# A transformer block on one core: the second attention with queries turned by DMA, its context prepared in the stage before, and an unrolled order

## The chip, the cores and the metric

The kernel runs on one core of a Trainium2 chip. The metric is device time in microseconds (us) of one execution; less is better. The core's engines run side by side, each through a queue of its own in program order, and wait for one another by semaphores: TensorE (PE, matmuls; PEld is its weight load), VectorE (DVE), ScalarE (ACT), GpSimd (POOL) and SyncE (SP), which here only issues DMAs. Sixteen DMA engines carry out all transfers.

## The reference, cut to what matters

The input is 32 batches of 256 rows by 256 numbers (x), and for each batch a context of 120 rows by 256. Four layers follow one another:

```python
x = x + tanh(g_xattn[0]) * attention_0(layernorm(x), ctx)          # with rope
x = x + tanh(g_ffn[0])   * mixture_of_8_experts(layernorm(x))      # top 2 of 8
x = x + tanh(g_xattn[1]) * attention_1(layernorm(x), ctx)          # gated
x = x + tanh(g_ffn[1])   * ternary_ffn_with_conv(layernorm(x))
```

The third one is rewritten. With 16 heads of 16 numbers it computes

```python
qn = layernorm(q) * qln_g + qln_b             # q is layernorm(x)
kk = (layernorm(ctx) * kvln_g + kvln_b) @ Wk.T;  vv = (the same) @ Wv.T
attn = softmax(q_heads @ k_heads.T / 4)       # q_ = qn @ Wq.T
y = attn @ v_heads
return (y * sigmoid(qn @ Wg.T + bg)) @ Wo.T
```

## The kernel before

`program` (the last function before the layouts) runs four blocks one after the other, each ended by a barrier of all engines: `attention_first`, `experts`, `attention_second`, `ternary_ffn`. P is 128, and a batch of 256 rows is held as two tiles of 128 rows. Where f32 precision is wanted from bf16 matmuls, an operand is split into a high bf16 half and the bf16 rest, and three products are summed (high by high, high by low, low by high): `halves`.

`attention_first` is unrolled over the batches (`unrolled`). Its queries and keys are turned by DMA transposes and the maxima are spread by a DMA.

`experts` works through 71 tiles of 256 sorted rows. SyncE loads a tile, transposes it by DMA into one of three buffers (`turn`, L1934 ff.), and stores results into `back_rows`. TensorE makes 54 bf16 matmuls for a tile (L2127). Between them, `early` loads and `prepare` get the weights of the next stages ready (in SBUF that lasts, `Early`).

`attention_second` (from L1207) handles one batch a period, in stages of a software pipeline: each engine has a hand-ordered list of pieces, and `at(k)` is the batch that entered k steps ago. `stepped` (L84) unrolls the first 8 steps, loops over pairs of batches, and unrolls the last 7. For one batch:

- SyncE loads x (`a_xa`, two buffers) and the places of its expert rows; GpSimd adds the two expert results of each row with four gathers (`indirect_dma_start`, L1359 and L1369). SyncE stores the sum to `x2_rows` (L1316) and loads it again as residual `a_xr` five steps later (L1304). It also loads the context (`a_ca`).
- VectorE computes the statistics of rows and context (L1489 to L1503), GpSimd the inverse root, VectorE the norm (L1529 rows, L1560 context).
- TensorE turns rows (four f32 transposes) and context (two, L1737); ScalarE scales them out of PSUM (L1458, L1401) and makes the high halves, GpSimd the low halves (L1342, L1344).
- TensorE makes queries (12 matmuls of 128x256), keys and values (6 of 120x512), gates (12). Queries and keys are laid out as `qx` and `kx`, 8 pairs of heads by 96 columns (high, high, low), by L1430, L1539, L1540 and L1432, L1542, L1543.
- TensorE turns `qx` in 16 transposes (L1666, L1676) and `kx` in 8 (L1672); ScalarE (L1453) and VectorE (L1551) copy the turned queries to `a_q`, VectorE the keys, masked for two heads (L1553, L1556).
- Eight pairs of matmuls `ms0` to `ms7` give the scores row by row, from which VectorE takes the negative maxima (the eight TENSOR_REDUCE). They are turned (L1651), copied by ScalarE (L1441, `mt`), and spread by VectorE over the eight pairs of heads in rows 96 to 127 of `a_q` (L1547). Eight pairs `sc0` to `sc7` then give scores less maxima, key by query, into two PSUM banks in turn; ScalarE takes each through Exp (the eight `a_probs`).
- 32 small matmuls multiply by the values (L1643, L1657), ScalarE copies (`raw`), TensorE turns back (L1705, L1709), VectorE divides by the sums (`a_of`), TensorE turns (`oT`), VectorE applies the gate (`a_ot`, L1513), TensorE projects with f32 `a_ot` and `wo` in 8 matmuls (in L1593, into `a_ps_a`), and VectorE adds the residual (L1474, `a_x`). SyncE stores.

`product` (L1589 ff.) issues all its matmuls from one line, so L1593 is queries, gates, keys and values, and projection; the output's name tells them apart (`a_ps_c`, `a_ps_d`, `a_ps_b`, `a_ps_a`).

## Time and profile before

| | us |
|---|---|
| median of 3 runs (lowest, highest) | 1911.04 (1910.23, 1912.43) |
| span of the profiled execution | 1909.9 |
| first attention, until its last store is issued | 0 to 507 |
| experts, until the last result is stored | to 973 |
| second attention | 974.7 to 1484.4 |
| ternary feed-forward | 1484.4 to 1909.9 |

The page of the profiled execution gives, over the whole span, TensorE 1671.7 us busy (88%), VectorE 1496.6 (78%), ScalarE 1330.9 (70%), GpSimd 1002.9 (53%). These are means over four stages with different limits, so the rows below are read stage by stage. In the timeline views a line gives start, length and engine of a group of like instructions; matmuls overlap, so what one costs is the distance of the starts, not its length.

### The profile page before, as it was taken

The page shows a single profiled execution, that of the slowest core. Times are in us where ns is not written, and L with a number is a line of the kernel's source. Part 1 is how long each engine was busy: PE and PEld are TensorE (multiplying, and loading weights), DVE is VectorE, ACT ScalarE, POOL GpSimd, SP SyncE. Part 2 cuts the span into 40 slices and gives each one's busy share as a digit, 9 for nine tenths or more (in the row PEclk, how much of TensorE's full clock was granted, in tenths as well). Part 3 has the DMA queues.
Part 4 walks back from the last instruction along what each step waited for, and adds up shares of the span by engine and source line. Part 5 has one row for each costly group of instructions (what it writes and reads, how often), then busy time and mean ns, then how long its engine had stood idle before and what let it go on. Part 6 is the DMA issues. An engine that isn't in the chain of part 4 may idle for free. (4 is left out here: it accounts for less than half of the span.)

```text
span 1909.9 us, 48511 instructions
## 1 busy us (share of the span) xinstructions
PE 1671.7 (88%) x15073; PEld 1387.0 (73%) x15073; DVE 1496.6 (78%) x4212; ACT 1330.9 (70%) x2855; POOL 1002.9 (53%) x1297
## 2 busy tenths in 40 slices
PE   4899999988649999999938999999999578888887
PEld 2677777766449999999936888888887366666666
DVE  5899999999544455333318999999996799999996
ACT  2788888878534444444416777777775599999997
POOL 5468888886733334333347766667660333333331
PEclk9999999999779999999969999999999799999999
DMA  7879999986577585555435555555551112222211
GB/s 230 211 174 216 207 205 224 204 194 186 167 188 204 135 143 136 137 140 138 119 78 105 118 115 116 120 120 111 118 121 40 56 50 66 66 66 66 64 54 48
DMA packets 407332, 250.90 MB, mean 131 GB/s; under 512 B 241647, under 2 KB 396783, under 8 KB 406151
## 3 DMA queue, kind: packets, MB, share of 16 engines
q1 hardware_dynamic: 381511, 213.14, 44.9%
q0 software_dynamic: 24576, 34.62, 9.1%
q8 instruction: 90, 1.47, 0.3%
q10 hardware_dynamic: 1088, 1.11, 0.2%
q14 instruction: 67, 0.55, 0.1%
HBM read 118.13 MB, written 74.30 MB: 101 GB/s over the span
## 5 line engine op out<-in xcount | busy, mean ns | idle before, releaser
L2127 PE MATMUL e_ps_ab<-e_turned,k_w_hi 128*128 128x256 bf16 (+1 forms) x1704 | 285.4, 274 | 23.1 <-DMA e_turned<-e_rows 23.1
L1981 POOL TENSOR_TENSOR e_h_lo<-e_h 128x256 bf16<-128x256 f32 (+1 forms) x213 | 139.4, 656 | 292.0 <-DVE e_h L2064 292.0
L2064 DVE TENSOR_TENSOR e_h<-e_s,e_ps_ab 128x256 f32<-128x256 f32 (+1 forms) x213 | 88.0, 415 | 221.1 <-ACT e_s L2003 221.1
L2127 PE MATMUL e_ps_ab<-e_turned,k_w_lo 128*128 128x256 bf16 (+1 forms) x852 | 233.5, 274 | 0.0
L2127 PEld LDWEIGHTS e_ps_ab<-e_turned,k_w_hi 128*128 (+1 forms) x1704 | 177.7, 107 | 38.1 <-issue 23.2
L2003 ACT ACTIVATE e_s<-e_ps_ab 128x256 f32<-128x256 f32 (+1 forms) x213 | 81.0, 382 | 118.6 <-PE e_ps_ab L2127 117.6
L2508 PE MATMUL f_ps_h<-f_qh,p_arena 128*128 128x256 bf16 x512 | 123.2, 280 | 35.7 <-DVE f_ql L2472 27.7
L2010 ACT ACTIVATE e_yo<-e_ps_y,e_xe 128x256 f32<-128x256 f32 x142 | 59.5, 470 | 113.8 <-PE e_ps_y L2127 113.8
L2508 PE MATMUL f_ps_h<-f_ql,p_arena 128*128 128x256 bf16 x512 | 122.3, 278 | 0.0
L2127 PE MATMUL e_ps_y<-e_w_hi,e_h 128*128 (+1 forms) x426 | 116.5, 273 | 1.0 <-POOL e_h_lo L1981 1.0
L2127 PE MATMUL e_ps_y<-e_w_hi,e_h_lo 128*128 (+1 forms) x426 | 115.9, 272 | 0.0
L2127 PE MATMUL e_ps_y<-e_w_lo,e_h 128*128 (+1 forms) x426 | 115.7, 272 | 0.0
L1359 POOL DMA_INDIRECT a_xa<-back_rows,a_where x64 | 107.2, 1676 | 15.7 <-issue 15.3
L2286 POOL TENSOR_TENSOR f_y<-f_y,f_tmp 128x510 f32<-128x510 f32 x32 | 43.6, 1362 | 136.7 <-DVE f_y L2407 136.7
L1369 POOL DMA_INDIRECT a_xa<-back_rows,a_where x64 | 99.7, 1558 | 22.1 <-issue 22.1
L2057 DVE TENSOR_TENSOR e_rows<-e_xe,e_rows 128x256 bf16<-128x256 f32 x142 | 78.2, 589 | 27.3 <-ACT e_rows L1997 27.2
L2127 PEld LDWEIGHTS e_ps_ab<-e_turned,k_w_lo 128*128 (+1 forms) x852 | 90.8, 107 | 7.1
L2508 PEld LDWEIGHTS f_ps_h<-f_qh,p_arena 128*128 128x128 bf16 x512 | 50.7, 99 | 61.6 <-DVE f_ql L2472 35.2
L519 POOL DMA_INDIRECT sent_rows<-k_xn,k_slot x64 | 64.0, 1000 | 23.9 <-issue 23.9
L560 POOL DMA_INDIRECT sent_rows<-k_xn,k_slot x64 | 64.6, 1010 | 19.4 <-issue 18.5
L977 PE MATMUL a_ps_b<-a_wo,a_ot 128*128 128x256 f32 x256 | 68.0, 412 | 1.4 <-ACT a_ot L635 1.4
L2508 PE MATMUL f_ps_y<-p_arena,f_zq 128*128 128x256 bf16 x512 | 61.1, 273 | 1.2 <-ACT f_zq L2351 1.2
(421 smaller groups left out, 6199.4 us busy)
## 6 DMA issues: line engine op xcount, KB each, us to landing
e_xe<-sent_rows SPq DMA_DIRECT2D x71, 272.0 KB, 2.9
back_rows<-e_yo SPq DMA_DIRECT2D x71, 256.0 KB, 2.1
x_rows<-a_x SPq DMA_DIRECT2D x64, 256.0 KB, 3.5
a_xa<-in_x SPq DMA_DIRECT2D x32, 256.0 KB, 3.3
p_arena<-in_xT SPq DMA_DIRECT2D x32, 256.0 KB, 3.4
a_xr<-in_x SPq DMA_DIRECT2D x32, 256.0 KB
a_xa<-x_rows SPq DMA_DIRECT2D x32, 256.0 KB, 3.3
x_rows<-a_xa SPq DMA_DIRECT2D x32, 256.0 KB, 2.3
```

What stands on the lines that cost most here:

```text
L519: nc.gpsimd.indirect_dma_start(sent[:, :], bass.IndirectOffsetOnAxis(ap=slot[:, b.quad, t, 0:1], axis=0), e_xn[:, b.quad, t, :], None).the ...
L560: nc.gpsimd.indirect_dma_start(sent[:, :], bass.IndirectOffsetOnAxis(ap=slot[:, b.quad, t, 1:2], axis=0), e_xn[:, b.quad, t, :], None).the ...
L977: last = nc.tensor.matmul(dst, l, r, start=(n == 0), stop=(n == len(terms) - 1))
L1359: nc.gpsimd.indirect_dma_start(xa[:, b.par, t, :], None, y_rows[:, :], bass.IndirectOffsetOnAxis(ap=where[:, b.par, 2 * t + 1:2 * t + 2], ...
L1369: nc.gpsimd.indirect_dma_start(xa[:, b.par, t, :], None, y_rows[:, :], bass.IndirectOffsetOnAxis(ap=where[:, b.par, 2 * t + 0:2 * t + 1], ...
L1981: nc.gpsimd.tensor_tensor(h_lo[0:k, b.par, c, :], h[0:k, b.par, c, :], h_hi[0:k, b.par, c, :], ALU.subtract).then_inc(mg.sem, 1)
L2003: nc.scalar.activation(s[0:k, b.par, c, :], ps_ab[0:k, bank(b, c), 0:N], ACT.Silu).then_inc(ma.sem, 1)
L2010: nc.scalar.activation(yo[:, b.par, t, :], ps_y[:, b.par, t * D:(t + 1) * D], ACT.Copy, scale=xe[:, b.n % XE, t, D:D + 1]).then_inc(my.sem, 1)
L2057: last = nc.vector.tensor_tensor(rows_[:, b.n % XR, 1, :, t, :], xe[:, b.n % XE, t, 0:D].rearrange("p (k n) -> p k n", k=KC), rows_[:, b.n ...
L2064: nc.vector.tensor_tensor(h[0:k, b.par, c, :], s[0:k, b.par, c, :], ps_ab[0:k, bank(b, c), N:2 * N], ALU.mult).then_inc(mh.sem, 1)
L2127: last = nc.tensor.matmul(to, left, right, start=(i == 0), stop=(i == len(terms) - 1))
L2508: last = nc.tensor.matmul(dst, l, r, start=(n == 0), stop=(n == len(terms) - 1))
```

## The change

1. Context. Its layer norm, with scale and shift now applied by row (`kvln`), its high and low halves and its transpose move into `experts`: a `context_...` piece on SyncE, VectorE, ScalarE and GpSimd in each of 64 tiles, one context every second tile (`context(n, first)`). The turned halves (128 x 512 bf16) are stored to `halves_c` and loaded in the second attention. Context statistics, norm, transposes, scaling and halves leave the second attention.
2. Queries. `qx` has 128 columns a pair (the last 32 zero, set once) and is turned by one DMA transpose a batch into one of three `q2` buffers; the 16 TensorE transposes and both copies go. The repeated high halves of q and k are copied by ScalarE instead of VectorE.
3. Maxima. They are spread by a DMA (128 KB) instead of by VectorE.
4. Output projection. `ot` is split in halves (high: the upper two bytes of the f32, read with a stride; low: a subtraction on GpSimd, `otl`), `wo` too (prepared in `experts`); 12 bf16 matmuls take the place of 8 f32 ones.
5. Rows. `xa` has eight buffers and is kept until the last sum; the store to and the load from `x2_rows` go.
6. Order. All 44 steps are unrolled (`Staged` semaphore counts), and every engine has a new list. VectorE computes the variance plus epsilon in one instruction instead of two on GpSimd. TensorE's list for one step is now: gates; keys turned; rows turned; raw halves turned (tb0, tb1); sc0 (waits for the spread's DMA), sc1; ms3, ms0; sc2; oT; sc3; sc6; ms2, ms1; projection; sc5; ms4, ms5; keys and values; ms7; sc4; ms6; sc7; queries; values times probabilities, first half; maxima turned; second half.

```diff
+def vacated(eng, *tenants):
+
+    for batch, *takers in tenants:
+        if batch is not None:
+            for signal, step in takers:
+                signal.wait(eng, batch, step)
+            return
+
...
+        xa = sb("xa", [P, 8, NT, D], F32)
...
+        def run(step):
+            for n in range(B + 13 - 1):
+                step(lambda s: Batch(n - s, (n - s) // 2, (n - s) % 2) if 0 <= n - s < B else None)
...
         @block.sync
         def _(sp):
+            sp.wait_ge(s_set, N_SET)
+
             def step(at):
+                b = at(2)
+                if b is not None:
+                    nc.sync.dma_start(chl[:, b.n % 3, :, :, :].rearrange("p h k s -> p (h k s)"), halves_c[b.n]).then_inc(c_ld[b.n % 3], 16)
+                b = at(0)
+                if b is not None:
+                    dve_out.wait(sp, at(8), "fin")
...
+                    nc.sync.dma_start(out_t[b.n], x1[:, b.n % 3, :, :]).then_inc(o_st[b.n % 3], 16)
                 b = at(5)
                 if b is not None:
-                    dve6.wait(sp, at(7), "fin")
-                    landed(sp, m_st, b)
-                    nc.sync.dma_start(xr[:, b.par, :, :], res_t[b.n]).then_inc(r_ld[b.par], 16)
-                b = at(0)
-                if b is not None:
-                    dve1.wait(sp, at(2), "norm")
-                    landed(sp, m_st, at(2))
-                    nc.sync.dma_start(xa[:, b.par, :, :], x_t[b.n]).then_inc(x_ld[b.par], 16)
-                    nc.sync.dma_start(where[:, b.par, :], places[b.n]).then_inc(w_ld[b.par], 16)
-                b = at(1)
-                if b is not None:
-                    dve1.wait(sp, at(3), "cnorm")
-                    nc.sync.dma_start(ca[0:S, b.par, :], a["ctx"][b.n]).then_inc(c_ld[b.par], 16)
-                    landed(sp, y_ld[1], b, NT)
-                    nc.sync.dma_start(res_t[b.n], xa[:, b.par, :, :]).then_inc(m_st[b.par], 16)
-                b = at(7)
-                if b is not None:
-                    dve6.wait(sp, b, "fin")
-                    nc.sync.dma_start(out_t[b.n], x1[:, b.par, :, :]).then_inc(o_st[b.par], 16)
-
-            run(nc.sync, step)
-            for par in range(2):
-                sp.wait_ge(o_st[par], 16 * B // 2)
-                sp.wait_ge(m_st[par], 16 * B // 2)
+                    act_keys.wait(sp, b, "mt")
+                    nc.sync.dma_start(q2[96:128, b.n % 3, :, :], mt[:, b.par, :].unsqueeze(1).to_broadcast([2 * H, NP, N])).then_inc(m_ld[b.n % 3], 16)
+                b = at(3)
+                if b is not None:
+                    act_rows.wait(sp, b, "q_hi2")
+                    dve_halves.wait(sp, b, "q_lo")
+                    nc.sync.dma_start_transpose(q2[:, b.n % 3, :, :].rearrange("p c (t n) -> p (c t) n", t=NT),
+                                                qx[:, b.par, :, :, :].rearrange("p c t k -> p (c t k)")).then_inc(q_ld[b.n % 3], 16)
...
+                    nc.gpsimd.tensor_tensor(xl[:, b.n % 3, :, :], xt[:, b.par, :, :], xh[:, b.n % 3, :, :], ALU.subtract).then_inc(gp_lows.sem, 1)
+                b = at(11)
+                if b is not None:
+                    dve_out.wait(gp, b, "ot")
+                    nc.gpsimd.tensor_tensor(otl[:, b.par, :, :], ot[:, b.par, :, :], ot_hi[:, b.par, :, :], ALU.subtract).then_inc(gp_lows.sem, 1)
...
-                    pe2.wait(act, b, "qTa")
-                    nc.scalar.activation(q2[0:96, b.par, 0:4, :].rearrange("p c n -> p (c n)"), ps_c[0:96, :].bitcast(BF16), ACT.Copy).then_inc(act2.sem, 1)
...
-                    act3.wait(dve, b, "mt")
-                    nc.vector.tensor_copy(q2[96:128, b.par, :, :], mt[:, :].unsqueeze(1).to_broadcast([2 * H, NP, N])).then_inc(dve3.sem, 1)
...
-                    pe2.wait(dve, b, "qTb")
-                    nc.vector.tensor_copy(q2[0:96, b.par, 4:8, :].rearrange("p c n -> p (c n)"), ps_d[0:96, :].bitcast(BF16)).then_inc(dve2.sem, 1)
...
+                b = at(10)
+                if b is not None:
+                    gp_lows.wait(pe, b, "otl")
+                    vacated(pe, (at(7),), (at(8),), (at(11), (dve_out, "fin")))
+                    for t in range(NT):
+                        last = product(ps_a[:, t * D:(t + 1) * D], halves(ot_hi[:, b.par, :, :], otl[:, b.par, :, :], slice(t * P, (t + 1) * P), woh, wol))
+                    last.then_inc(pe_out.sem, 1)
...
+                if b is not None:
+                    arrived(pe, c_ld, b)
+                    vacated(pe, (at(9),), (at(5), (act_rows, "xt")))
+                    product(ps_b[0:S, :], halves(chl[:, b.n % 3, 0, :, :], chl[:, b.n % 3, 1, :, :], slice(0, S), wkvh, wkvl, 0, 2 * D)).then_inc(pe_keys.sem, 1)
...
-                        last = product(ps_a[:, t * D:(t + 1) * D], terms(ot, slice(t * P, (t + 1) * P), wo))
...
+            def context_load(c):
+                if c is not None:
+                    if c.n:
+                        cv.wait(sp, contexts[c.n - 1], "stats")
+                    cl.wait(sp, contexts[c.n - 2] if c.n >= 2 else None, "lo")
+                    sp.dma_start(c_rows[0:S, c.par, :], a["ctx"][c.n]).then_inc(c_ld, 16)
+
+            def context_turn(c):
+                if c is not None:
+                    cl.wait(sp, c, "lo")
+                    if c.n >= 2:
+                        sp.wait_ge(c_st, 16 * (c.n - 1))
+                    nc.sync.dma_start_transpose(c_turned[:, c.par, :, :, :].rearrange("p h k n -> p (h k) n"),
+                                                c_half[:, c.par, :, :].rearrange("p h d -> p (h d)")).then_inc(c_tr, 16)
+
+            def context_store(c):
+                if c is not None:
+                    sp.wait_ge(c_tr, 16 * (c.n + 1))
+                    if c.n:
+                        sp.wait_ge(c_st, 16 * c.n)
+                    sp.dma_start(halves_c[c.n], c_turned[:, c.par, :, :, :].rearrange("p h k n -> p (h k n)")).then_inc(c_st, 16)
 
...
+                if b.n == 0:
+                    sp.dma_start(c_norm[:, :, :].rearrange("p g d -> p (g d)"), a["kvln"]).then_inc(c_ld, 16)
+                    sp.wait_ge(c_ld, 16)
+                context_store(context(b.n, 8))
+                context_turn(context(b.n, 6))
+                context_load(context(b.n, 1))
                 if b.n == 20:
...
+            def context_high(c):
+                if c is not None:
+                    cv.wait(act, c, "normed")
+                    if c.n >= 2:
+                        act.wait_ge(c_tr, 16 * (c.n - 1))
+                    nc.scalar.activation(c_half[0:S, c.par, 0, :], c_rows[0:S, c.par, :], ACT.Copy).then_inc(cs.sem, 1)
...
+            def context_root(c):
+                if c is not None:
+                    dve.wait_ge(c_ld, 16 * (c.n + 2))
+                    nc.vector.bn_stats(c_stats[0:S, :], c_rows[0:S, c.par, :]).then_inc(cv.sem, 1)
+                    cv.wait(dve, c, "stats")
+                    nc.vector.bn_aggr(c_mv[0:S, :], c_stats[0:S, :]).then_inc(cv.sem, 1)
+                    cv.wait(dve, c, "mv")
+                    nc.vector.tensor_scalar(c_ve[0:S, :], c_mv[0:S, 1:2], EPS, None, ALU.add).then_inc(cv.sem, 1)
+
+            def context_norm(c):
+                if c is not None:
+                    cg.wait(dve, c, "root")
+                    nc.vector.scalar_tensor_tensor(c_rows[0:S, c.par, :], c_rows[0:S, c.par, :], c_mv[0:S, 0:1], c_norm[0:S, 0, :],
+                                                   ALU.subtract, ALU.mult).then_inc(cv.sem, 1)
+                    cv.wait(dve, c, "scaled")
+                    nc.vector.scalar_tensor_tensor(c_rows[0:S, c.par, :], c_rows[0:S, c.par, :], c_root[0:S, 0:1], c_norm[0:S, 1, :],
+                                                   ALU.mult, ALU.add).then_inc(cv.sem, 1)
+
+            def context_low(c):
+                if c is not None:
+                    cs.wait(dve, c, "hi")
+                    nc.vector.tensor_tensor(c_half[0:S, c.par, 1, :], c_rows[0:S, c.par, :], c_half[0:S, c.par, 0, :], ALU.subtract).then_inc(cl.sem, 1)
```

## Rows read from the trace of the kernel before

**Rows 1.** Busy time per engine in steady stretches: columns, then clock, DMA share, GB/s.

```profile
core 0: us, PE busy (x) PEld busy (x) DVE busy (x) ACT busy (x) POOL busy (x), PEclk, DMA share, GB/s
150.00:400.00 250.00, 239.93 (x2176) 183.39 (x2175) 248.45 (x900) 204.70 (x523) 209.57 (x306) 1.00 0.95 212
600.00:900.00 300.00, 300.00 (x2748) 274.62 (x2747) 130.67 (x271) 135.27 (x360) 101.91 (x154) 1.00 0.61 139
1086.30:1375.00 288.70, 288.70 (x2922) 243.68 (x2920) 273.91 (x681) 218.88 (x460) 198.79 (x221) 1.00 0.54 118
```

**Rows 2.** Timeline: start, length of the last sum, first batch and two neighbours.

```profile
1052.94 0.75 DVE L1474 SCALAR_TENSOR_TENSOR a_x<-a_ps_a,p_half_tg,a_xr 128x512 f32<-128x512 f32 x1
...
1096.30 0.75 DVE L1474 SCALAR_TENSOR_TENSOR a_x<-a_ps_a,p_half_tg,a_xr 128x512 f32<-128x512 f32 x1 [0.17 <-PE a_ps_a L1593]
...
1125.17 0.75 DVE L1474 SCALAR_TENSOR_TENSOR a_x<-a_ps_a,p_half_tg,a_xr 128x512 f32<-128x512 f32 x1 [0.16 <-PE a_ps_a L1593]
```

**Rows 3.** TensorE's timeline inside one period of the second attention.

```profile
1206.23 0.65 PE L1666 MATMUL a_ps_d<-p_identb,a_qx 128*96 128x128 bf16 x8
1206.72 0.59 PE L1672 MATMUL a_ps_a<-p_identb,a_kx 120*96 120x120 bf16 x8
1207.14 0.61 PE L1676 MATMUL a_ps_c<-p_identb,a_qx 128*96 128x128 bf16 x8
1207.59 0.38 PE L1684 MATMUL a_ps_e<-a_q,p_arena 128*120 128x256 bf16 x2
...
1209.77 1.90 PE L1593 MATMUL a_ps_a<-p_arena,a_ot 128*128 128x256 f32 x8
1211.50 0.37 PE L1737 MATMUL a_ps_b<-p_ident,a_cn 120*128 120x120 f32 x2
1211.71 0.38 PE L1743 MATMUL a_ps_e<-a_q,p_arena 128*120 128x256 bf16 x2
...
1212.57 0.27 PE L1593 MATMUL a_ps_d<-a_xh,p_arena 128*128 128x256 bf16 x1
...
1213.88 0.38 PE L1778 MATMUL a_ps_e<-a_q,p_arena 128*120 128x256 bf16 x2
```

**Rows 4.** Busy time by stretch in the fill and drain, columns as in rows 1.

```profile
974.60:994.30 19.70, 0.00 (x0) 0.00 (x0) 2.21 (x10) 0.00 (x0) 11.58 (x18) 0.50 0.45 86
994.30:1009.00 14.70, 6.72 (x32) 4.31 (x32) 3.63 (x14) 3.83 (x8) 12.70 (x14) 0.56 0.52 104
1009.00:1024.00 15.00, 11.06 (x107) 8.64 (x108) 14.07 (x34) 8.88 (x18) 10.44 (x14) 1.00 0.54 101
...
1456.00:1470.00 14.00, 12.47 (x110) 9.53 (x109) 8.88 (x19) 8.28 (x16) 0.00 (x0) 1.00 0.13 39
1470.00:1484.40 14.40, 8.23 (x68) 5.70 (x66) 3.90 (x8) 2.87 (x6) 0.00 (x0) 1.00 0.24 73
```

**Rows 5.** The experts' weight loads from e_h: ns least, median, most.

```profile
L2127 PEld LDWEIGHTS e_ps_y<-e_w_hi,e_h x426: 95/98/181, 559.7 to 970.6; 128*128 128x128 bf16 x142
```

**Rows 6.** Groups by shape, 1086 to 1376: busy us, mean ns, idle before.

```profile
L1551 DVE COPY a_q<-a_ps_d 96x1024 bf16<-96x1024 bf16 x20 | 13.7, 687 | 2.5
L1547 DVE COPY a_q<-a_mt 32x2048 bf16<-32x2048 bf16 x20 | 13.7, 687 | 0.6
...
L1359 POOL DMA_INDIRECT a_xa<-back_rows,a_where x40 | 67.7, 1693 | 9.5 <-issue 9.5
...
L1342 POOL TENSOR_TENSOR a_xl<-a_xt,a_xh 128x512 bf16<-128x512 f32 x20 | 35.0, 1751 | 0.0
```

**Rows 7.** First attention: us to landing of two DMAs, SyncE's ns for one.

```profile
a_q<-a_mt SPq DMA_DIRECT2D x32, 128.0 KB, 2.4
...
a_q<-a_qx SPq DMA_TRANSPOSE x32, 5.7
...
L465 SPq DMA_TRANSPOSE a_q<-a_qx x32: 1592/2774/5190, 34.2 to 461.0; - x32
```

**Rows 8.** Timeline in the drain: a bare chain of score pair and exponential.

```profile
1469.04 0.43 PE L1778 MATMUL a_ps_e<-a_q,p_arena 128*120 128x256 bf16 x2 [0.47 <-ACT a_probs L1395]
...
1469.51 0.60 ACT L1410 ACTIVATE a_probs<-a_ps_e 120x512 f32<-120x512 f32 x1
```

893 lines of the change are left out of this document (429 added, 464 removed).

## The prediction, made before the changed kernel was run

> **What bounds the kernel now.** I read the busy times by stage first, because the change touches two of the four stages: the experts, which only get small work added, and the second attention, which is rewritten. [rows 1] shows one steady stretch of each of the first three stages, with the sum of busy time beside the stretch. In the experts (600 to 900) TensorE is busy for all of the 300 us while VectorE, ScalarE and GpSimd are under half, so small work on those three is covered as long as nobody makes TensorE wait. In the second attention (1086 to 1375) TensorE is again busy for 288.7 of 288.7 us, but VectorE with 273.9 is close behind it (95%), ScalarE has 219 and GpSimd 199. In the first attention, which already has the shape the second one is to get (transposes by DMA, the order unrolled), VectorE is the full one (248 of 250) and TensorE has 240.
>
> Second, the length of one period of the second attention: the starts of its last step, the sum x + gate, are in [rows 2]. From 1096.30 to 1125.17 are two batches, 28.87 us, so 14.44 us for one. The first of all is at 1052.94.
>
> Third, whether "busy" is real: in TensorE's timeline of one period [rows 3] each group starts where the one before leaves off. I add the starts' distances for one batch: query and gate products 1.31 us each, keys and values 1.38, eight score pairs at 0.22 (1.73), eight pairs for the maxima at 0.21 (1.66), probabilities times values with the turning of the maxima 1.96, turns of rows, output and the two raw halves 0.43 + 0.43 + 0.90, keys turned 0.42, queries turned 0.49 + 0.45, context turned 0.21, output projection 1.73. That is 14.41 us against the period of 14.44: TensorE is fed without a gap, and its instructions alone set the period. So what leaves TensorE shortens the period until the next limit.
>
> Last, the ends of the stage [rows 4]: it runs from 974.6 (its first load) to 1484.4 (its last store has landed and the next stage loads), 509.8 us. 32 periods of 14.44 are 462.1, so 47.7 us are overhead: 19.7 before TensorE starts, about 12 idle and some slowed instructions (granted clock 0.56, which is mostly the lower of the two levels, 1.2 GHz) in 994 to 1024, and about 8 in the two last windows, with the last sum and store.
>
> **The change on TensorE.** Removed for each batch: the sixteen turns of the queries, 1206.23 to 1206.72 and 1207.14 to 1207.59, 0.94 us; the two turns of the context, 1211.50 to 1211.71, 0.21 us. The output projection was eight f32 matmuls, 1209.77 to 1211.50, 1.73 us; it becomes twelve bf16 ones of the same shape as the gate's, which take 1212.57 to 1213.88, 1.31 us [rows 3]. It saves 0.42. Its stationary operand is every second bf16 of an f32 tile; the experts load such an operand (e_h read in halves) in 98 ns, under the matmul's own 109, so I price the stride at nothing [rows 5]. Sum: 1.57 us less, a period of 12.87 us if TensorE stays fed, and 32 x 1.57 = 50 us for the stage.
>
> The Trainium skill would price the projection otherwise: FP8 and Floating Point Precision, TensorE Precision Notes, gives true FP32 four passes through the array. By that rule the eight old matmuls would be 8 x 4 x 0.109 = 3.5 us and the swap would save 2.2 us a batch, 57 us more in all. The row has 1.73 us, two passes' worth, and the row decides.
>
> **The other engines.** VectorE loses the spread of the maxima over eight pairs (0.69 us), the copy of half of the turned queries (0.69) [rows 6], and the copies of q and k, which go to ScalarE, and the context's statistics and norm: 2.8 us of 13.7 a batch, so 10.9 to 11.1 are left with the small new "ve". ScalarE loses the other half of the query copy and three operations on the context and gets two copies: about 1.3 us less than its 10.9. GpSimd loses one context subtraction and two small operations, and gets the low half of the gated output; the same subtraction for the rows costs 1.75 us here [rows 6]. It goes from 9.9 to about 10.5 to 11.5 of 12.87. No engine is above the period, but GpSimd and VectorE are at four fifths and more of it, and each runs in a fixed order.
>
> **The queue of SyncE.** Two things move there from engines. The queries' transpose is a DMA: in the first attention it holds the queue for 2.8 us (median; up to 5.2) and lands after 5.7 us, the spread of the maxima is a second DMA that lands after 2.4 us [rows 7]. Behind the transpose stand the next batch's loads and the store; they have eight buffers of rows now, so nobody waits for them. The turned queries are needed by the maxima more than a period after they are written: covered. The spread is not: TensorE turns the maxima just before the second half of probabilities times values, and the first score pair, which needs the landed spread, comes after that half, the gate, the keys' and rows' turns and the two raw halves: 0.97 + 1.31 + 0.42 + 0.43 + 0.90 = 4.0 us. ScalarE's copy (0.4) and the landing (2.4) with gaps make 3.1. So it is hidden with 0.9 us to spare; gone is the wait on VectorE that the old order had. The bytes are no limit: store and load of the residual and the raw context go (2 x 256 + 120 KB), 128 KB of prepared context, the 512 KB transpose and the spread come. The DMA engines are busy for 0.54 of the stretch now and for 0.95 in the first attention, where two such transposes run in a batch of 13 us [rows 1].
>
> **What the order costs.** The new order packs the scores differently. From the first score pair to the fifth TensorE has four pairs, two pairs of maxima and one turn, 1.7 us; but on one PSUM bank the chain is pair, exponential, pair, exponential, pair. [rows 8] has a bare chain: pair at 1469.04, exponential at 1469.51, 0.47 later; it takes 0.60, and with 0.05 for the signal the next pair on that bank follows 0.65 after its start. Twice this is 2.24 us, so TensorE can stand still for up to 0.5 us a period. The new queue of VectorE has keys' halves, statistics and reciprocals close ahead of what TensorE needs at its step's start, with a tenth or two to spare. Between 0 (the old order lost nothing) and 1.0 I take 0.3, near the first end, since the old order lost nothing by the same kind of chain: 27 full periods, 8 us.
>
> **Fill and drain.** TensorE's steps span six stages instead of five, VectorE's seven instead of six, and in the fill and the drain the landings of transpose and spread have no cover: a transpose (5.7) once in the fill where a turn with its copy took about 1.5, a spread about 3 us in each of two or three steps of the fill and of the drain. Against that, less TensorE work is strung through these steps. The old fill and drain idled about 20 us in [rows 4]; I add 8 us (2 to 16). All engines also wait for VectorE to clear the queries' buffer before the first load: 1 us.
>
> **The experts.** Every second tile now has a context load, a transpose half the size of the tile's own, a store, and about 2 us of small operations on VectorE. TensorE's feed has three turned tiles in hand. SyncE first waits for the small table to land, about 3 us at the first tile. I take +1 us (0 to 6). The last context is stored at the last tile but one, so the stage's end does not move.
>
> **The sum.** Profiled span 1909.9 - 50.3 + 8 + 8 + 1 + 1 = 1877.6 us. The median of the runs is 1.1 us above the profiled span, and I keep this distance: 1879 us.
>
> **Rivals.**
> 1. TensorE stays fed and the deeper pipeline costs almost nothing. For it: the old order lost 0 us in twenty periods. Against: the score chain above and the uncovered landings. 1877.6 - 8 - 6 = 1864, with the distance 1865.
> 2. Another engine's order sets the period. GpSimd's four gathers at 1.7 us [rows 6] with 0.3 between them, root, and two subtractions at up to 1.75 make a ring of 11.5 to 12.5 us, VectorE has 11; with the waits of the one for the other that would give a period of about 13.7 instead of 13.2: 27 x 0.5 = 14 us above the forecast, about 1893 us. For it: VectorE is full in the first attention [rows 1].
> 3. The landing of the spread takes the place of the turns, and the kernel gets slower. Every batch waits there, and the wait adds wholly to the period. The cover is 4.0 us. Of the 50.3 us gained 10 go for fill, drain, start and experts in any case; the other 40.3 are used up at 1.5 us a period, so the kernel is slower from a way of 4.0 + 1.5 = 5.5 us on, instead of 3.1. That happens if the spread's packets stand behind a gather's, or the copy behind ScalarE's key and query copies. In the first attention, with busier DMA engines, the landing has median 2.4, which speaks against it. At 5.8 us it would be 27 x 1.8 = 49 us, and 1909.9 - 50.3 + 49 + 10 + 1.1 = 1920 us.
> 4. The change does not do what it says: the bf16 projection is no faster, as its loads of strided weights are not hidden. Then only 1.15 us a batch go: 1879 + 13 = 1892 us, inside the range.
>
> **Chances.** Forecast 1879 (1871 to 1888) 0.52; rival 1, 0.14; rivals 2 and 4, 0.24; no change 0.03; rival 3, 0.07. To hold 8 in 10 the range goes from 1863 to 1898. A difference under 0.2% (3.8 us) is about what a measurement of this kernel cannot tell from none. Faster 0.90, same 0.03, slower 0.07.
>
> **What would show it.** The distance of two batches' last sums in the second attention is 26.2 to 26.6 us (28.87 now); 25.8 would be rival 1, 27 and more rival 2. TensorE's groups: twelve matmuls of the projection in 1.3 us, no turns of queries or context. TensorE's idle time is put down to exponentials before the fifth pair; rival 3 shows as TensorE waiting for the DMA of the maxima before the first pair in every batch. The stage is 476 to 480 us, its first sum 78 to 88 us after its first load (78.3 now). The experts keep their length, with TensorE busy for the whole of it; if it is not, the context's work sits in its way and I was wrong there. The feed-forward stage keeps its length.

## The result, and the profile after

The changed kernel takes 1899.61 us (median of 5 runs, 1896.22 to 1901.71) against 1910.23 us for the one before on the same chip: ratio 0.9936, 95% interval 0.9921 to 0.9951. So it is faster, by 0.6%, but not by the 1.6% forecast: 1899.6 is 20.6 us above the 1879 of the prediction and 1.6 us above the end of its range. The profiled execution, the fastest of the five, has a span of 1894.4 us; 1877.6 was forecast (each run that is listed with both has its time 1.8 us above its span).

The stages, by the first operation of each (GpSimd's small memset, 974.67 and 1484.4 before, 977.17 and 1468.7 after): experts end 2.5 us later (+1 forecast), second attention 491.5 us and not 509.7 (-18.2; forecast -33.3), feed-forward 425.7 against 425.5 (no change forecast). 0.2 + 15.1 + 1.5 = 16.8 us is the distance of the two spans.

The 2.5 us hide two parts. A line of TensorE's second products in the experts (`e_ps_y`) gives their first and last start, before and after:

```profile
L2127 PE MATMUL e_ps_y<-e_w_hi,e_h x426: 269/273/283, 559.7 to 970.7; 128*128 x142
L2165 PE MATMUL e_ps_y<-e_w_hi,e_h x426: 270/273/282, 556.9 to 973.2; 128*128 x142
```

These are 411.0 us before and 416.3 here, so the experts themselves take 5.3 us more. The other 2.8 us go the other way and lie in the first attention, whose code is the same: its last sum starts anywhere from 501.1 to 508.5 us in the fourteen profiles of this case (505.9 before, 503.1 here).

First the busy times of after by stretch, which answer to [rows 1]; the columns are the stretch, its length, busy time of each engine, TensorE's granted clock, share of the DMA engines, GB/s:

```profile
600.00:900.00 300.00, 296.62 (x2714) 271.23 (x2712) 187.98 (x420) 141.45 (x381) 117.72 (x178) 1.00 0.75 170
650.00:700.00 50.00, 46.62 (x425) 42.25 (x424) 32.18 (x62) 24.69 (x62) 16.65 (x24) 1.00 0.83 150
1096.69:1364.29 267.60, 265.81 (x2642) 214.07 (x2641) 223.51 (x560) 205.25 (x420) 191.62 (x181) 1.00 0.75 139
1000.00:1050.00 50.00, 32.64 (x195) 19.67 (x196) 26.11 (x62) 19.18 (x40) 34.25 (x32) 0.68 0.60 100
```

TensorE is no longer busy for the whole of these 300 us of the experts: 3.4 us are missing, all of them from 650 to 700. In twenty periods of the second attention (third row) it is busy for 265.8 of 267.6 us. The last row is in the fill, at a granted clock of 0.68.

Second the last sums of a batch in the second attention (VectorE's timeline), which answer to [rows 2]:

```profile
1069.92 0.75 DVE L1488 SCALAR_TENSOR_TENSOR a_x<-a_ps_a,p_half_tg,a_xa 128x512 f32<-128x512 f32 x1 [0.29 <-PE a_ps_a L1566]
...
1096.69 0.75 DVE L1488 SCALAR_TENSOR_TENSOR a_x<-a_ps_a,p_half_tg,a_xa 128x512 f32<-128x512 f32 x1 [0.30 <-PE a_ps_a L1566]
1110.07 0.75 DVE L1488 SCALAR_TENSOR_TENSOR a_x<-a_ps_a,p_half_tg,a_xa 128x512 f32<-128x512 f32 x1 [0.29 <-PE a_ps_a L1566]
...
1465.31 0.75 DVE L1488 SCALAR_TENSOR_TENSOR a_x<-a_ps_a,p_half_tg,a_xa 128x512 f32<-128x512 f32 x1 [1.65 <-PE a_ps_a L1566]
```

A period is 13.38 us (14.44 before, 13.17 forecast); the first sum comes 92.7 us after the stage's first operation (78.3 before, 78 to 88 forecast); from the first to the last are 395.4 us.

Third, TensorE's timeline of one period, which answers to [rows 3], from the first score pair to the projection:

```profile
1279.68 0.38 PE L1610 MATMUL a_ps_e<-a_q,p_arena 128*120 128x256 bf16 x2
1279.90 0.38 PE L1614 MATMUL a_ps_e<-a_q,p_arena 128*120 128x256 bf16 x2
1280.11 0.37 PE L1622 MATMUL a_ps_m<-p_arena,a_q 96*128 96x240 bf16 x2
1280.32 0.37 PE L1627 MATMUL a_ps_m<-p_arena,a_q 96*128 96x240 bf16 x2
1280.75 0.43 PE L1635 MATMUL a_ps_e<-a_q,p_arena 128*120 128x256 bf16 x2
1281.01 0.60 PE L1573 MATMUL a_ps_b<-p_ident,a_of 128*128 128x128 f32 x4
1281.45 0.38 PE L1646 MATMUL a_ps_e<-a_q,p_arena 128*120 128x256 bf16 x2
1281.86 0.43 PE L1651 MATMUL a_ps_e<-a_q,p_arena 128*120 128x256 bf16 x2
1282.13 0.37 PE L1658 MATMUL a_ps_m<-p_arena,a_q 96*128 96x240 bf16 x2
1282.34 0.37 PE L1664 MATMUL a_ps_m<-p_arena,a_q 96*128 96x240 bf16 x2
1282.54 0.38 PE L1566 MATMUL a_ps_a<-p_arena,a_ot 128*128 128x256 bf16 x2
...
1283.85 0.38 PE L1679 MATMUL a_ps_e<-a_q,p_arena 128*120 128x256 bf16 x2
```

The projection takes 1283.85 - 1282.54 = 1.31 us, as priced. A pair of maxima takes 0.21, but the one at 1280.32 is followed by 0.43, and the score pair at 1281.45 (0.22) by 0.41: two gaps of 0.2 us. The two score pairs that waited (1280.75 and 1281.86) then take 0.27 each, where others take 0.22. Together this is 0.51 us, all that the period has above the 12.87 forecast for TensorE's own instructions. The gaps do not show as idle time of PE, because the printed ends of matmuls overlap the next ones. The weight loads show them; from TensorE's waits, 1150 to 1350, 15 periods (total, times, longest):

```profile
...
PEld a_ps_e L1635 <- ACT a_probs L1439: 4.9, 15, 0.3
PEld a_ps_e L1651 <- ACT a_probs L1445: 3.9, 14, 0.3
PEld a_ps_e L1742 <- ACT a_probs L1395: 3.2, 15, 0.2
```

The longest line of this list, left out here, is the load for the first gate matmul (6.2 us, which the profile puts down to nobody); the gates take 1.32 us where they took 1.31, so it costs next to nothing. The third line shown, ahead of the probabilities times values, is no loss. TensorE takes 1.40 us from the start of the queries (1286.64) to it where the queries' own matmuls take 1.31, but experiment 2 has the same 1.40 with no exponential to wait for, and before, keys and values took 1.39 ahead of these matmuls and take 1.30 now. So the 0.09 us belong to the 14.41 us of before.

And ScalarE's timeline beside it:

```profile
1280.10 0.60 ACT L1439 ACTIVATE a_probs<-a_ps_e 120x512 f32<-120x512 f32 x1
1280.59 0.59 ACT L1442 ACTIVATE a_probs<-a_ps_e 120x512 f32<-120x512 f32 x1
1281.21 0.60 ACT L1445 ACTIVATE a_probs<-a_ps_e 120x512 f32<-120x512 f32 x1
```

This is the bare chain of [rows 8], twice: pair 1279.68, exponential 1280.10, next pair on that bank 1280.75, exponential 1281.21, next pair 1281.86.

Last, the fill. TensorE's turns of the rows (once a step), and its waits from 974 to 1070:

```profile
996.57 1.12 PE L1573 MATMUL a_ps_b<-p_ident,a_xn 128*128 128x128 f32 x4 [22.88 <-DVE a_xn L1538]
1011.45 1.11 PE L1573 MATMUL a_ps_b<-p_ident,a_xn 128*128 128x128 f32 x4 [2.10 <-DVE a_xn L1538]
1021.69 1.07 PE L1573 MATMUL a_ps_b<-p_ident,a_xn 128*128 128x128 f32 x4
1035.69 0.61 PE L1573 MATMUL a_ps_b<-p_ident,a_xn 128*128 128x128 f32 x4
1051.29 0.61 PE L1573 MATMUL a_ps_b<-p_ident,a_xn 128*128 128x128 f32 x4
1064.22 0.61 PE L1573 MATMUL a_ps_b<-p_ident,a_xn 128*128 128x128 f32 x4
```

```profile
...
PE a_ps_c L1566 <- POOL a_xl L1336: 8.9, 1, 8.9
...
PE a_ps_e L1610 <- DMA a_q<-a_mt: 0.9, 1, 0.9
```

The steps of the fill are 14.9, 10.2, 14.0, 15.6 and 12.9 us long (15.8, 11.6, 14.0, 13.3 and 14.4 before). The first sum comes 4.0 us after the fifth turn before, and 5.7 us after the sixth one here.

### The profile page after: what moved, and what is told of

Its sections match the earlier page's. It is cut to its first block and busy times, and to the rows that moved or that the text cites. A ratio compares the mean times of both kernels' runs of the same rounds, so it can differ in the third digit from the quotient of the medians.

```text
span 1894.4 us, 45159 instructions
## 1 busy us (share of the span) xinstructions
PE 1642.1 (87%) x14625; PEld 1340.3 (71%) x14625; DVE 1492.7 (79%) x4215; ACT 1318.3 (70%) x2823; POOL 1017.1 (54%) x1262
## 5 line engine op out<-in xcount | busy, mean ns | idle before, releaser
L1351 POOL DMA_INDIRECT a_xa<-back_rows,a_where x64 | 101.9, 1593 | 15.3 <-issue 15.2
L1360 POOL DMA_INDIRECT a_xa<-back_rows,a_where x64 | 99.9, 1562 | 15.1 <-issue 15.1
L570 POOL DMA_INDIRECT sent_rows<-k_xn,k_slot x64 | 64.7, 1011 | 18.9 <-issue 15.8
L1344 POOL TENSOR_TENSOR a_rstd<-a_ve,a_half 128x2 f32<-128x2 f32 x32 | 23.3, 728 | 75.7 <-DVE a_ve L1525 75.4
```

The source lines that it names most:

```text
L570: nc.gpsimd.indirect_dma_start(sent[:, :], bass.IndirectOffsetOnAxis(ap=slot[:, b.quad, t, 1:2], axis=0), e_xn[:, b.quad, t, :], None).the ...
L1351: nc.gpsimd.indirect_dma_start(xa[:, b.n % 8, t, :], None, y_rows[:, :], bass.IndirectOffsetOnAxis(ap=where[:, b.n % 3, 2 * t + 1:2 * t + ...
L1360: nc.gpsimd.indirect_dma_start(xa[:, b.n % 8, t, :], None, y_rows[:, :], bass.IndirectOffsetOnAxis(ap=where[:, b.n % 3, 2 * t + 0:2 * t + ...
```

## The experiments

Each time is a median. The kernel before took 1909.5 to 1911.7 us beside the four groups of experiments. The changed kernel was run once more, beside the second group:

> The changed kernel once more, as the measure for its neighbours of this call: 1896 to 1902 us, the second attention's first load at 977 to 981 us, last sums 13.38 us apart. All theories expect the same of it.

It took 1898.5 us (ratio 0.9940, 0.9927 to 0.9954; profiled span 1895.4), and I measure by that. The four groups ran on different chips, and the kernel before differs by 2.2 us between them, so a difference in us between two groups is no surer than that; each ratio is against the kernel before on the same chip.

**1. The period: projection moved between the score pairs.**

```diff
+                    product(ps_a[:, 0:D], halves(ot_hi[:, b.par, :, :], otl[:, b.par, :, :], slice(0, P), woh, wol))
                 b = at(8)
                 if b is not None:
                     act_probs.wait(pe, b, "ex0")
...
+                    product(ps_a[:, D:2 * D], halves(ot_hi[:, b.par, :, :], otl[:, b.par, :, :], slice(P, 2 * P), woh, wol)).then_inc(pe_out.sem, 1)
+                b = at(8)
+                if b is not None:
                     act_probs.wait(pe, b, "ex2")
```

> The output projection (1.31 us) leaves its place after the second pair of maxima; its first half stands between the fourth and the fifth pair of that stretch, ahead of the score pair that waits for exponential 0, its second half ahead of the score pair that waits for exponential 2. Theory A (the 0.51 us that a period of 13.38 us has above TensorE's 12.87 are two bare chains of pair, exponential, pair on one PSUM bank): both gaps close, last sums are 12.9 to 13.0 us apart, 27 periods give 10 to 12 us, the kernel takes 1888 to 1890 us. Theory B (another engine's ring, GpSimd's gathers or VectorE's order, holds the period near 13.4): the gaps move to other waits and the time stays within 3 us of 1899.6. Theory C (the move itself delays the turned output and with it VectorE): slower than 1900.

1907.6 us, ratio to before 0.9991 (0.9978 to 1.0004), 9 us slower than the changed kernel. The period is 13.73 us. TensorE's waits, 1150 to 1350, and a line of VectorE's timeline:

```profile
PE a_ps_m L1689 <- DVE a_mneg L1479: 4.9, 15, 0.3
PE a_ps_m L1695 <- DVE a_mneg L1482: 2.8, 15, 0.2
```

```profile
1275.30 0.66 DVE L1479 TENSOR_REDUCE a_mneg<-a_ps_m 128x4 f32<-128x480 f32 x1 [0.61 <-PE a_ps_m L1668]
```

The waits for exponentials 0 and 2 are gone from the list, so the chains are what the 0.2 us gaps were. But two pairs of maxima came behind both halves of the projection. VectorE stood idle 0.61 us for them, and the next pairs now wait for its reductions. Theory C named the wrong operation (not the turned output, but the maxima), in the right direction.

**2. The same with the maxima left in their place.** The order from score pair 2 on is: pair 2, turn of the output, maxima, pair 3, maxima, pair 6, second half, pair 5. On ScalarE the last exponential goes ahead of the copy of the keys.

```diff
+                b = at(7)
+                if b is not None:
+                    dve_tops.wait(pe, b, "top0")
...
                 b = at(8)
                 if b is not None:
                     act_probs.wait(pe, b, "ex1")
...
-                    dve_tops.wait(pe, b, "top0")
...
+                b = at(8)
+                if b is not None:
+                    act_probs.wait(pe, b, "ex2")
```

> The projection split again, but the two pairs of maxima that VectorE's reductions wait for keep their place in time: first half of the projection ahead of score pair 2, the turn of the output, maxima, score pair 3, maxima, score pair 6, second half of the projection, score pair 5. On ScalarE the last exponential goes ahead of the copy of the keys' high half. Theory A (in the first split both bare chains of exponentials were covered, and the new loss came only from the reductions that started 0.6 us late): last sums 13.0 to 13.15 us apart, 27 periods give 6 to 10 us against 13.38, the kernel takes 1889 to 1894 us. Theory B (any order loses half a microsecond a period somewhere, since VectorE's reductions and ScalarE's exponentials alternate with TensorE on two banks each): 13.3 us or more, no gain of over 2 us.

1885.9 us, ratio 0.9878 (0.9863 to 0.9893): 12.6 us below the changed kernel, a little more than the 6 to 10 expected. The last sums (VectorE's timeline) and what is left of the waits between 1150 and 1350:

```profile
1083.55 0.74 DVE L1488 SCALAR_TENSOR_TENSOR a_x<-a_ps_a,p_half_tg,a_xa 128x512 f32<-128x512 f32 x1
1096.59 0.74 DVE L1488 SCALAR_TENSOR_TENSOR a_x<-a_ps_a,p_half_tg,a_xa 128x512 f32<-128x512 f32 x1
```

```profile
...
PEld a_ps_m L1697 <- DVE a_mneg L1482: 3.7, 15, 0.2
PEld a_ps_e L1747 <- issue: 3.4, 16, 0.2
```

13.03 us, 0.35 less, with the same instructions. 13.03 is the 12.87 of TensorE's own instructions and one remaining wait: a pair of maxima ahead of L1697 takes 0.35 us instead of 0.20. The second line stands where the changed kernel had its third wait (probabilities times values). It is as long as before, but no exponential ends it any more. From the first to the last sum it is 384.6 against 395.4 us.

**3. The projection back to true f32** (GpSimd's low half still computed and waited for):

```diff
-                        last = product(ps_a[:, t * D:(t + 1) * D], halves(ot_hi[:, b.par, :, :], otl[:, b.par, :, :], slice(t * P, (t + 1) * P), woh, wol))
+                        last = product(ps_a[:, t * D:(t + 1) * D], [(ot[:, b.par, c, t * P:(t + 1) * P], wo[:, c, :]) for c in range(KC)])
```

> The changed kernel with the output projection as true f32 matmuls again, on the same tiles; GpSimd still computes the low half and TensorE still waits for it, only nobody reads it. Theory A (TensorE's instructions and the two bare exponential chains set the period): the group takes 1.73 us and not 1.31, last sums are 13.8 us apart, 31 intervals give 12 to 13 us, the kernel takes 1910 to 1912 us, so that the whole change would have brought nothing. Theory B (the period has slack elsewhere and the projection stands in it): last sums still 13.4 us apart, under 3 us.

1913.0 us, ratio 1.0013 (0.9997 to 1.0029). The period (VectorE's timeline):

```profile
1076.92 0.75 DVE L1489 SCALAR_TENSOR_TENSOR a_x<-a_ps_a,p_half_tg,a_xa 128x512 f32<-128x512 f32 x1 [0.72 <-PE a_ps_a L1567]
1090.72 0.75 DVE L1489 SCALAR_TENSOR_TENSOR a_x<-a_ps_a,p_half_tg,a_xa 128x512 f32<-128x512 f32 x1 [0.72 <-PE a_ps_a L1567]
```

13.80 us, 0.42 more: the price taken from [rows 3], to the hundredth. The median rises by 14.5 us, 31 x 0.42 = 13.0 of it from the periods. The prediction's aside on the Trainium skill (FP8 and Floating Point Precision, TensorE Precision Notes: four passes for true FP32) miscounted, though. The line issues four f32 matmuls (not eight, as the text ahead has it), two row tiles by two halves of the sum, and the profile shows each as two entries, hence x8 in [rows 3]. Four of four passes at 0.109 us are 1.74 us, and the row has 1.73: trace and rule agree, and "3.5 us" was my error. The sum went by the row and is not touched.

**4. The experts: no context work** (no load, norm, split or turn, only the stores, of a constant; the second attention's keys and values are therefore not the reference's):

```diff
-            return contexts[k // 2] if k >= 0 and k % 2 == 0 and k // 2 < B else None
+            return contexts[k // 2] if first == 8 and k >= 0 and k % 2 == 0 and k // 2 < B else None
```

> The experts load, turn, normalise and split no context; only the store of each context's block is left, of a constant. The second attention computes with that constant, so all its later results are left out; its instructions are the same. Theory A (the experts are 3.2 us longer than before because context loads that land late hold VectorE's queue around the placement table's transfer): the second attention's first load comes 2 to 4 us earlier, at 974 to 976 us, and TensorE is busy for 50 of 50 us from 650 to 700; the kernel takes 1896 to 1898 us. Theory B (it is run to run spread of the experts): no change of the start beyond 1 us.

1890.6 us, ratio 0.9902 (0.9886 to 0.9919), 8 us less than the changed kernel where 2 to 4 were expected. The second attention begins at 972.3; the ten profiles with the changed kernel's context work (after, again, experiments 1 to 3 and 6 to 10) have 977.2 to 983.7, median 979.1. TensorE's products from 557.3 to 968.3 take 411.0 us, exactly as before the change, and it is full again from 650 to 700:

```profile
650.00:700.00 50.00, 50.00 (x461) 45.91 (x459) 27.79 (x51) 25.22 (x61) 19.08 (x26) 1.00 0.80 151
```

Where the time sits in the changed kernel, by SyncE's queue and VectorE's timeline:

```profile
677.23 0.58 SPq L1957 DMA_DIRECT2D places<-e_placed  x1
678.25 4.93 SPq L1897 DMA_TRANSPOSE e_turned<-e_rows  x1
...
685.74 0.45 SPq L1910 DMA_DIRECT2D k_xn<-in_ctx  x1
```

```profile
682.62 0.81 DVE L2071 TENSOR_TENSOR e_h<-e_s,e_ps_ab 128x256 f32<-128x256 f32 x2
691.06 0.43 DVE L2122 BATCH_NORM_STATS2 k_xn<-k_xn 120x6 f32<-120x256 f32 x1 [7.64 <-DMA k_xn<-in_ctx]
```

A transpose holds SyncE for 4.93 us, the context load behind it is issued late, and VectorE, which has the context's statistics next in its queue, waits 7.64 us for it. Behind the statistics stands the product (`e_h`) that TensorE needs, directly and through GpSimd's low half of it. TensorE's waits from 545 to 972 in the changed kernel:

```profile
...
PE e_ps_y L2165 <- POOL e_h_lo L1970: 3.7, 3, 1.4
PE e_ps_ab L2165 <- DVE e_h L2071: 1.9, 1, 1.9
```

**5. A third buffer for the context,** and its work one tile later:

```diff
-                    cl.wait(sp, contexts[c.n - 2] if c.n >= 2 else None, "lo")
+                    cl.wait(sp, contexts[c.n - 3] if c.n >= 3 else None, "lo")
...
-                context_root(context(b.n, 2))
-                context_norm(context(b.n, 3))
+                context_root(context(b.n, 3))
+                context_norm(context(b.n, 4))
```

> The experts' context rows get a third buffer, and all work on a context comes one tile later than its load than it did, so that the load has two tiles (12 us) instead of one to land. Nothing is left out. Theory A (TensorE's losses in the experts, 3.4 us from 650 to 700 and 1.3 to 2.4 us from 550 to 600, come from VectorE's queue waiting for a context load of its own tile): these windows are back at 50 of 50 and about 49, VectorE waits for context loads for under 5 us in all (51.6 us with two buffers), the second attention starts 3 to 5 us earlier than with two buffers, the kernel takes 1892 to 1896 us. Theory B (the small operations themselves cost the time): the start moves by under 1 us, and the kernel stays at 1898 to 1901 us.

1890.0 us, ratio 0.9892 (0.9877 to 0.9907). VectorE's waits for the load from 545 to 972, the changed kernel first, then this one, and TensorE's stretch and second products here:

```profile
DVE k_xn L2122 <- DMA k_xn<-in_ctx: 51.6, 31, 7.6
```

```profile
DVE k_xn L2128 <- DMA k_xn<-in_ctx: 6.5, 2, 3.7
```

```profile
600.00:900.00 300.00, 300.00 (x2747) 274.90 (x2746) 188.18 (x425) 142.66 (x385) 117.11 (x179) 1.00 0.79 172
```

```profile
L2171 PE MATMUL e_ps_y<-e_w_hi,e_h x426: 269/273/281, 559.8 to 970.9; 128*128 x142
```

The same operations (VectorE busy 188.18 against 187.98 us) without the wait: TensorE is full, and its products take 411.0 us (970.86 - 559.82), as before the change, in experiment 4 and in experiment 11. The ten profiles with two buffers have 416.3 to 422.4 us, median 419.1. So it was the wait and not the work, and the wait costs 5.3 us in the profile of the result and 8.1 at the median. The median time gains 8.5 us (4 to 8 were expected). The profiled spans differ by 3.9 only (1895.4 to 1891.5), because in this profile the unchanged first attention ends 3.2 us later (505.7 against 502.5). Two things were changed at once here, the buffer and the order; which of them alone would do was not tried.

**6. The fill: TensorE kept at work in its idle time** (matmuls that nobody reads, 266 in all):

```diff
+            def keep(k):
+                for _ in range(k):
+                    nc.tensor.matmul(ps_e[:, 0, 0:N], identb[:, :], wqh[:, 0, 0:N], start=True, stop=True)
+
+            keep(145)
```

> Fills TensorE's idle time in the first steps of the second attention with matmuls that nobody reads: 145 before its first turn, 18 before the second batch's turn, 75 before the first queries, 20 and 8 before the turns of the first two batches' keys. Theory A (the fill is long because TensorE's instructions run at the lower clock after its idle time): the window from first load to first sum, 92.0 us, shrinks by 4 to 8 us, the kernel takes 1892 to 1896 us. Theory B (the fill is long because a batch passes through one more step and each step lasts as long as GpSimd's gathers and the chain of maxima let it): under 2 us change, 1898 to 1901 us. Theory C (the extra matmuls stand in the way): slower by up to 5 us.

1900.4 us, ratio 0.9953 (0.9937 to 0.9969). The granted clock from 1000 to 1050 rises from 0.68 to 0.90, and the first sum comes 91.0 us after the first operation; the two profiles of the changed kernel have 92.7 and 91.6. TensorE's first turn comes 0.8 us later than there, so the clock was worth 1.5 to 2.6 us of the fill from there on, and nothing of it shows in the kernel's time.

**7. Half of the gathers left out** (the second expert's rows are not added):

```diff
-                        nc.gpsimd.indirect_dma_start(xa[:, b.n % 8, t, :], None, y_rows[:, :],
-                                                     bass.IndirectOffsetOnAxis(ap=where[:, b.n % 3, 2 * t + 1:2 * t + 2], axis=0),
-                                                     compute_op=ALU.add).then_inc(y_ld[b.n % 3], 16)
```

> The second attention gathers and adds only the first expert's rows; the second pair of gathers of each batch is left out, so its rows lack that term. GpSimd's work per batch falls by 3.9 us. Theory A (GpSimd's four gathers a step set the length of the steps in the fill): the window from first load to first sum shrinks from 92.0 us by 8 to 16 us; the steady distance of last sums stays 13.38 us. Theory B (the fill's steps are set by the chain through TensorE, ScalarE and VectorE): the window shrinks by 2 to 5 us only. Theory C (GpSimd's ring sets the period): the steady distance falls too, by 0.3 us or more, and the kernel by 10 us or more over the fill's share.

1889.8 us, ratio 0.9916 (0.9889 to 0.9942). The first sum comes after 83.9 us, 8.8 less; the period stays at 13.38. Of the 8.8, 3.4 are ahead of TensorE's first turn (993.5 - 977.5 = 16.0 against 19.4) and 4.8 in the next two steps (11.0 and 9.3 against 14.9 and 10.2). So gathers set the first steps of the fill (before the change these were 15.8 and 11.6 long; there it was not tested), and GpSimd does not set the period. Nor does TensorE's list of waits in the steady stretch name VectorE: rival 2 is out.

**8. The low halves of the first three batches between the gathers:**

```diff
+                b = at(6)
+                if b is not None and b.n < 3:
+                    act_rows.wait(gp, b, "xh")
+                    nc.gpsimd.tensor_tensor(xl[:, b.n % 3, :, :], xt[:, b.par, :, :], xh[:, b.n % 3, :, :], ALU.subtract).then_inc(gp_lows.sem, 1)
                 b = at(4)
```

> In the second attention GpSimd computes the low halves of the rows of the first three batches between its two pairs of gathers, and not behind both. Theory A (in the first steps TensorE's queries wait for a low half that stands behind gathers: 8.9 us at the first batch): first sum 2 to 5 us earlier after the first load than 92 us, the kernel takes 1895 to 1898 us. Theory B (the fill's length is the number of steps by the chain through the maxima): under 1 us.

1898.3 us, ratio 0.9946 (0.9932 to 0.9959). First sum after 91.0 us (91.6 in the profile of the changed kernel run beside it). The wait of 8.9 us for GpSimd, the largest in the list, was worth 0.6 us at most, less than the 1.2 by which the two profiles of the changed kernel differ. The first step shrinks from 15.0 to 11.7 us, and the second grows from 10.4 to 12.1; what holds that one was not followed.

**9. One step fewer.** Keys and values in the step of the batch's own queries, everything behind them a step earlier:

```diff
-        pe_keys = Staged(sem(tag + "pe_keys"), "kT:7 kv:6 mT:7")
+        pe_keys = Staged(sem(tag + "pe_keys"), "kT:6 kv:5 mT:6")
```

> The changed kernel with one step fewer between a batch's rows and its keys: keys and values are computed in the step of the batch's own queries, and everything behind them comes one step earlier; the order within a step is the same. Nothing is left out. Theory A (the changed kernel's fill is one step, 13 to 14 us, longer since the queries' transposition, 6.5 us to landing plus two copies, needs a step of its own to hide in): first sum 10 to 15 us earlier than the 92 us after the first load, but TensorE now waits 2.5 to 3.5 us in every batch for the transposed queries ahead of the first maxima, last sums 15.8 to 17 us apart, the kernel 50 to 90 us slower than with the extra step. Theory B (the extra step was not needed): the fill is shorter and the period stays at 13.4 to 13.6, the kernel takes 1885 to 1890 us. Theory C (the fill is set by gathers and the chain of maxima): first sum under 5 us earlier.

2046.9 us, ratio 1.0713 (1.0681 to 1.0744). TensorE's waits from 1150 to 1350:

```profile
PE a_ps_m L1622 <- DMA a_q<-a_qx: 37.4, 11, 4.1
```

It waits in each of the 11 periods, 3.4 us for the transposed queries, and the periods are 17.3 to 21.3 us long, worse than theory A had it; what the rest of a period goes to was not followed. The first sum comes 98.9 us after the first operation, not earlier: in the fill, too, the transposed queries are waited for (13.2 us in four batches). The step is needed; its price could not be read from this run.

**10. One step more,** with the buffers for it (rows 9, turned queries, halves and contexts 4):

```diff
-        pe_keys = Staged(sem(tag + "pe_keys"), "kT:7 kv:6 mT:7")
+        pe_keys = Staged(sem(tag + "pe_keys"), "kT:8 kv:7 mT:8")
```

> The changed kernel with one step more between a batch's queries and its keys, and one more buffer of rows, of halves, of turned queries and of contexts for it; the order within a step is the same. Nothing is left out. Theory A (a step of the pipeline costs its full length in the fill and little in the drain, since TensorE's instructions go in order and the steps of the fill last 13 to 15 us whether TensorE is full or not): last sums stay 13.38 us apart, the first one comes 12 to 14 us later than the 92 us after the first load, the kernel takes 1910 to 1913 us. This would also be the price of the step that the changed kernel has over the one before. Theory B (a step of the fill costs only what its landings leave uncovered, the rest being strung into it): first sum 3 to 8 us later, the kernel 1902 to 1906 us.

1910.3 us, ratio 0.9988 (0.9974 to 1.0003), 11.9 us slower. The period stays at 13.38; the first sum:

```profile
1085.63 0.75 DVE L1488 SCALAR_TENSOR_TENSOR a_x<-a_ps_a,p_half_tg,a_xa 128x512 f32<-128x512 f32 x1 [0.29 <-PE a_ps_a L1566]
```

It comes 1085.6 - 981.1 = 104.5 us after the first operation, 12 to 13 later, and from first to last sum are 394.3 us (395.4). This further step costs its full length in the fill and nothing in the drain.

**11. Order of 2 and buffer of 5 together.** The two edits are those shown above; nothing else is changed.

> The order of the second split (projection in halves, maxima left in place) together with the third context buffer. Nothing is left out. If the two are independent, last sums are 13.03 us apart as with the order alone, TensorE is full from 600 to 900 as with the buffer alone, and the gains of 12.6 and 8.5 us add: 1876 to 1880 us. If the third buffer's gain was partly chance of the run, 1881 to 1885 us.

1877.8 us, ratio 0.9822 (0.9799 to 0.9846), 1.8% faster than before the change. The last sums are 13.03 us apart, TensorE is busy for 300 of 300 us in the experts. The two gains add, within what two groups can be compared to (21.1 expected, 20.7 measured).

## Why the prediction was wrong, point by point

**TensorE's content was right.** Turns of queries and context are gone, the projection takes 1.31 us, strided weights cost nothing, so rival 4 is out; experiment 3 gives the 0.42 back. Only the aside that set the skill's four passes against the row was wrong, as told there. The content of 12.87 us is confirmed by the changed kernel's timeline (13.38 less the 0.51 of the gaps) and by experiment 2, whose one wait of 0.15 us is what it has above 12.87.

**The order's price was mis-sized: 0.51 us a period and not 0.3.** The step that failed is the choice inside the bound. The text computed the chain (2.24 us against 1.7 of cover, up to 0.5) and then took 0.3 "since the old order lost nothing by the same kind of chain". The old order said nothing about this one: it had other work between the pairs. The chain's arithmetic held (up to 0.5): 0.41 us in two gaps, and 0.1 in the two score pairs behind them. Nor did it hold for only 27 periods: the intervals from first to last sum shrank by 428.0 - 395.4 = 32.6 us, which is, up to 0.3, 31 x 1.57 = 48.7 of content less 31 x 0.51 = 15.8. The forecast had 50.3 - 8 = 42.3, so 9.7 are missing. Of these 5.7 us are the size of the gap (27 x 0.21), 2.0 the four periods more and 1.6 the 32nd batch, which has no interval of its own.

**Fill, drain and start: +14.4 us against +9, and by another mechanism.** The first sum comes 92.7 us after the stage's first operation and not 78.3; drain and end are as before (in the drain the sums come closer together than a period, by 31 x 13.38 - 395.4 = 19.4 us in all, before by 31 x 14.44 - 428.0 = 19.6). I had added up uncovered landings. But TensorE waits 0.9 us for the spread in the whole fill and never for the transposed queries: what costs is the step itself, which is there to cover the transposition (experiment 9). Experiment 10 prices a further step of this kind at 12 to 13 us; that the first one cost the same is inferred from it, and that this is most of the 14.4. "Less TensorE work is strung through these steps" was no relief: a step of the fill lasts 10 to 16 us although TensorE is busy for only 33 of the 50 us from 1000 to 1050. Gathers set the first two (experiment 7); clock and low halves are worth 2.6 us and 0.6 us at most (6, 8). That the chain through reductions and copies does is argued from the waits, not shown, and so are the last 1.5 to 2.5 of the 14.4 us. With the 9.7 above these 5.4 make the stage's 15.1 us.

**The experts: right in sign, wrong in cover.** The stage takes 5.3 us more in the profile and 8.1 at the median of ten, against +1 (0 to 6), and the reason was missing. I looked at SyncE's queue and TensorE's three tiles in hand, and not at VectorE's: a wait for a DMA at the head of its queue stops the products behind it. Without it the experts are as long as before the change, and the kernel took 8.5 us less (experiment 5). That the end of the stage moved by only 2.5 us was luck: the unchanged first attention ended 2.8 us earlier in this profile.

**The distance of span and median was assumed.** I kept 1.1 us; the profiled run was the fastest of five, and the distance is 5.2. Its experts are also the shortest of the ten, by 2.8 us under the median, which may be most of the 3.4 us by which it is faster than the median run; the other runs have no trace to show it. Together: 15.1 in the second attention, 4.3 in the experts, -2.8 in the first attention, 0.2 in the feed-forward stage and 4.1 here are 20.9 us, the 20.6 of the miss up to rounding.

**The rivals.** 1 (fully fed) fell by 0.51 us a period. 2 had a period of 13.7 by GpSimd's ring, and GpSimd has no part in it (experiment 7): it is busy for 9.6 us of 13.38, less than the 10.5 to 11.5 estimated, since its two subtractions take 1.16 and 1.04 us and not the 1.75 of before. Experiment 1 has a period of 13.73, but by the maxima that VectorE waits for. 3 did not happen: no wait for the spread in the steady stretch. 4 did not happen either; its 1892 us lay outside the range of 1871 to 1888, not inside as the text has it. VectorE with 11.2 us a batch and ScalarE with 10.3 were forecast as 11 and 9.6.

## What to carry to other kernels

Where two engines alternate on one PSUM bank, add up pair, signal, exponential and signal from a row, lay it against the work that the new order puts between the pairs, and take that number: an order that lost nothing in the old kernel is no evidence for the new one. Such a gap can be filled with any work whose inputs are old (the projection here), but what another engine waits for must not move back with it, or the gap reappears larger (13.73 us for 13.38 in experiment 1). A load that is consumed in the queue of an engine which also feeds the bottleneck needs slack of its own, and where a DMA in place of an on-chip copy needs a pipeline step to hide its landing, that step has a price of its own, here about 12 us once per launch.

## What the runs showed of the hardware

TensorE's busy share hides gaps of 0.2 us: in the twenty periods it is busy for 265.8 of 267.6 us, yet 20 x 0.51 = 10.2 us are lost, because a group's last matmul is drawn some 0.16 us into the next group (0.38 us for a pair that starts 0.22 us ahead of the next). Only starts and the waits of the weight loads show them.

An f32 matmul stands in the profile as two entries, as the eight of the projection for four issued show, while an f32 transpose stands as one (x4 for the four turns of the rows); a count of entries is not a count of instructions.

A transpose by DMA of a tile's 256 rows held SyncE for 1.26 us (median of 71) and for 4.93 us at 678.25, right behind the transfer of the placement table. Before the change it was 3.67 us at the same place, so the hold is not new; new is the context load that stands behind it.
